# A decoder layer's router, tile by tile in place of pairs of tiles

## The reference, cut to what matters

```
x = layernorm(x + attn(x) @ Wo)                 # norm a
r = running sum over the batch of decay, ctx*ctx
x = layernorm(x + x * r)                        # norm b, written here in one product x * (r + 1)
h = rmsnorm(x) * norm_w
scores = softmax(h @ gate_w)                    # 32 experts
topk_w, topk_ids = top_k(scores, 4); topk_w /= sum(topk_w)
pos = rank of the token among those of the same expert, in token order
buf[expert, pos] = h, where pos < 256           # the rest is dropped
shared = silu(h @ shared_gate) * (h @ shared_up) @ shared_down
```

## Time and profile before

| | us |
|---|---|
| median of 3 runs | 1106.15 |
| lowest and highest | 1100.98, 1106.28 |
| the profiled execution | 1102.41 |
| its span | 1100.5 |

### The profile page before, as it was taken

The page is one execution under the profiler, slowest core; times in us unless marked ns, Lnnn a source line. Parts: engine busy times, 40 slices in busy tenths (PEclk is TensorE's granted clock), DMA queues, the critical chain, the costliest instruction groups (busy, mean ns, idle before and its releaser), DMA issues. The chain is left out here.

```text
span 1100.5 us, 18924 instructions
## 1 busy us (share of the span) xinstructions
PE 999.9 (91%) x6064; PEld 816.0 (74%) x6064; DVE 712.1 (65%) x2102; ACT 606.8 (55%) x1650; POOL 461.0 (42%) x473
## 2 busy tenths in 40 slices
PE   7999999998995699849899999988878889999996
PEld 5999899987883599727778888965444568877775
DVE  6666766672575366545655767645777557888886
ACT  3655566556222255436676776656775546555553
POOL 5777767861367444366211110210137214444321
PEclk9999999999997799969999999998988989999999
DMA  6731111000011599733401101001003011112101
GB/s 214 252 132 66 29 30 29 16 15 2 1 49 55 186 351 331 251 96 109 135 20 63 30 26 39 1 23 51 2 1 117 1 58 58 58 58 66 51 1 39
DMA packets 83784, 85.61 MB, mean 78 GB/s; under 512 B 8577, under 2 KB 75975, under 8 KB 83568
## 3 DMA queue, kind: packets, MB, share of 16 engines
q1 hardware_dynamic: 79776, 75.59, 21.1%
q0 software_dynamic: 3072, 7.34, 2.2%
q10 hardware_dynamic: 848, 1.57, 0.4%
HBM read 63.36 MB, written 22.02 MB: 78 GB/s over the span
## 5 line engine op out<-in xcount | busy, mean ns | idle before, releaser
L579 POOL TENSOR_TENSOR a_qk<-h,a_by_sin 128x512 f32<-128x512 f32 x64 | 81.9, 1279 | 5.0
L352 DVE CUSTOM_DVE_ANT_0 h<-a_score_ps,mask_bf 128x128 f32<-128x128 f32 (+1 forms) x128 | 40.8, 355 | 60.0 <-PE a_score_ps L345 60.0
L1296 POOL TENSOR_TENSOR a_w_l<-a_w,a_w_h 128x256 fp32r<-128x256 f32 x30 | 21.9, 729 | 111.2 <-ACT a_w_h L1489 111.0
L358 ACT ACTIVATE y_moe<-y_moe,a_nmax 128x128 f32<-128x128 f32 x64 | 25.6, 400 | 76.1 <-DVE a_nmax L352 76.1
L339 DVE COPY a_probsT<-a_turn_ps 128x384 f32<-128x384 f32 x64 | 34.9, 545 | 48.2 <-PE a_turn_ps L269 48.2
L1035 POOL TENSOR_TENSOR e_w_l<-e_w,e_w_h 128x512 fp32r<-128x512 f32 x32 | 40.8, 1275 | 52.7 <-ACT e_w_h L1103 52.7
L459 PEld LDWEIGHTS a_proj_ps<-a_w,xT 128*128 128x128 f32 x512 | 59.6, 192 | 1.3 <-issue 0.5
L80 PE MATMUL a_proj_ps<-a_x_l,a_w_h 128*128 128x512 f32 x128 | 56.9, 445 | 3.7 <-POOL a_w_l L584 3.6
L459 PE MATMUL a_proj_ps<-a_w,xT 128*128 128x128 f32 x512 | 59.8, 276 | 0.1
L759 PE MATMUL t_y_ps<-wo,attnT 128*128 128x256 f32 x256 | 57.6, 381 | 0.0
L2639 POOL TENSOR_TENSOR m_up_l<-m_up_w,m_up_h 128x1024 fp32r<-128x1024 f32 x8 | 19.5, 2438 | 89.3 <-ACT m_up_h L2611 89.3
(11 more groups left out here) (465 smaller groups left out, 3519.7 us busy)
## 6 DMA issues: line engine op xcount, KB each, us to landing
slots<-zeros SPq DMA_DIRECT2D x4, 2048.0 KB, 7.0
e_rows<-slots SPq DMA_DIRECT2D x32, 256.0 KB, 4.5
e_w<-in_L_ffn_w_dram SPq DMA_DIRECT2D x32, 256.0 KB, 4.7
out_slots<-e_out SPq DMA_DIRECT2D x32, 256.0 KB, 4.2
e_w<-in_L_ffn_w_dram SPq DMA_DIRECT2D x32, 128.0 KB, 4.1
a_w<-in_L_attn_w_q_dram SPq DMA_DIRECT2D x32, 128.0 KB, 2.2
m_up_w<-in_up_dram SPq DMA_DIRECT2D x8, 512.0 KB, 3.6
a_w<-in_L_attn_Wq_dram SPq DMA_DIRECT2D x16, 128.0 KB, 2.2
```

Of the source, the lines that this page charges most:

```text
L352: done = dve.tensor_tensor_reduce(self.probs[:, b, cells], self.score_ps[:, r, cells], self.k.mask_bf[:, cells], -1.0, 3e38, ALU.add, ALU. ...
L358: act.activation(self.probs[:, b, 0:P], self.probs[:, b, 0:P], ACT.Exp, bias=self.nmax[:, b, 0:1], scale=-1.0, accum_out=self.total[:, b, ...
L579: pool.tensor_tensor(qk[:, par, 0 if what == "q" else 1, half * HALF:(half + 1) * HALF], by_cos[:, r, :], by_sin[:, r2, :], ALU.add).then_ ...
```

## The change

The router's functions treat one tile each. `centre(t)` only finds the largest logit, and ScalarE's `exp` reads the logits in PSUM with it as bias, so that the subtraction (line 812) is gone. `place` makes its four products by one instruction over 128 elements. In VectorE's loop `choose(t - 2)` and `place(t - 2)` stand in every turn from t = 2, and `centre(t - 1)` from t = 1; all of `weigh` moves behind the loop. On TensorE `count(t - 3)` and `logits(t - 2)` stand in every turn. On GpSimd the scatters of tile t - 3 are issued in turn t from t = 3. Behind the loop the second shared product is cut into two halves, with the last count between them.

```diff
-                def logits(g):
-                    pe.wait_ge(k.hT_ready, 2 * g + 2)
-                    at_least(pe, centred, g)
-                    for t in (2 * g, 2 * g + 1):
+                def logits(t):
+                    pe.wait_ge(k.hT_ready, t + 1)
...
-                def shared_up(half):
-                    pe.wait_ge(k.hT_ready, 4 * half + 4)
+                def shared_up(half, j):
+                    if j == 0:
+                        pe.wait_ge(k.hT_ready, 4 * half + 4)
...
-                        if h == 11 and t >= 3 and t % 2:
-                            logits((t - 3) // 2)
-                        if h == 9 and t >= 4 and t % 2 == 0:
-                            count((t - 4) // 2)
+                        if h == 9 and t >= 3:
+                            count(t - 3)
+                        if h == 11 and t >= 2:
+                            logits(t - 2)
...
-                shared_up(0)
+                shared_up(0, 0)
+                shared_up(0, 1)
+                count(5)
                 turn_h(6)
-                count(2)
+                logits(6)
+                count(6)
                 turn_h(7)
-                logits(3)
-                shared_up(1)
-                count(3)
+                logits(7)
+                shared_up(1, 0)
+                count(7)
+                shared_up(1, 1)
...
-                def choose(g):
-                    ts = slice(2 * g, 2 * g + 2)
-                    dve.wait_ge(scored, g + 1)
-                    for t in (2 * g, 2 * g + 1):
-                        last = dve.max(top[:, t, :], score[:, t, :])
-                    chain(last)
-                    for t in (2 * g, 2 * g + 1):
-                        last = dve.max_index(top_at[:, t, :], top[:, t, :], score[:, t, :])
-                    chain(last)
+                def choose(t):
+                    dve.wait_ge(scored, t + 1)
+                    chain(dve.max(top[:, t, :], score[:, t, :]))
+                    chain(dve.max_index(top_at[:, t, :], top[:, t, :], score[:, t, :]))
...
                     residual(t)
-                    if t >= 3 and t % 2:
-                        choose((t - 3) // 2)
+                    if t >= 2:
+                        choose(t - 2)
                     if t >= 1:
                         rms(t - 1)
                     decay_gate(t)
-                    if t >= 3 and t % 2:
-                        place((t - 3) // 2)
+                    if t >= 2:
+                        place(t - 2)
+                    if t == NT - 1:
+                        centre(t - 1)
                     ln_b.gate(dve, t)
-                    if t >= 2 and t % 2 == 0:
-                        centre((t - 2) // 2)
+                    if 1 <= t < NT - 1:
+                        centre(t - 1)
                     ln_b.apply(dve, t)
-                    if t >= 4 and t % 2 == 0:
-                        weigh((t - 4) // 2)
+                choose(6)
                 rms(7)
-                centre(3)
-                choose(3)
-                place(3)
-                weigh(2)
-                weigh(3)
+                place(6)
+                for t in range(4):
+                    weigh(t)
+                centre(7)
+                choose(7)
+                weigh(4)
+                weigh(5)
+                place(7)
+                weigh(6)
+                weigh(7)
...
-                    if t == 4:
+                    if t == 3:
                         pool.wait_ge(k.zeroed, ZERO_DMAS * 16)
-                    if t >= 4:
-                        scatter(t - 4, (0, 1, 2))
+                    if t >= 3:
+                        scatter(t - 3, (0, 1, 2))
                     ln_b.power(pool, t)
-                    if t >= 4:
-                        scatter(t - 4, (3,))
+                    if t >= 3:
+                        scatter(t - 3, (3,))
                 rms_power(7)
-                for t in range(4, NT):
+                for t in range(5, NT):
                     scatter(t)
```

More of the change, by code:

```diff
@@ L731, in count @@
-                def count(g):
-                    pe.wait_ge(masked, g + 1)
-                    at_least(pe, slots_ready, g)
-                    for t in (2 * g, 2 * g + 1):
-                        for u in range(t + 1):
-                            last = pe.matmul(pos_ps[:, t * E0:(t + 1) * E0], (k.before_bf if u == t else k.ones_bf)[:, :],
-                                             mask[:, u, :], start=u == 0, stop=u == t)
-                    last.then_inc(counted, 1)
-                def shared_up(half):
-                    pe.wait_ge(k.hT_ready, 4 * half + 4)
[L742 to L748, removed]
+                def logits(t):
+                    pe.wait_ge(k.hT_ready, t + 1)
+                    for c in range(DC):
+                        last = pe.matmul(logit_ps[:, t * E0:(t + 1) * E0], k.hT[:, c, t * P:(t + 1) * P],
+                                         k.gate_w[:, c, :], start=c == 0, stop=c == DC - 1)
+                    last.then_inc(logits_done, 1)
@@ new lines, in count @@
+                def count(t):
+                    pe.wait_ge(masked, t + 1)
+                    for u in range(t + 1):
+                        last = pe.matmul(pos_ps[:, t * E0:(t + 1) * E0], (k.before_bf if u == t else k.ones_bf)[:, :],
+                                         mask[:, u, :], start=u == 0, stop=u == t)
+                    last.then_inc(counted, 1)
+                def shared_up(half, j):
+                    if j == 0:
+                        pe.wait_ge(k.hT_ready, 4 * half + 4)
+                        if half:
+                            pe.wait_ge(ln_a.summed, NT)
+                    for c in range(DC):
+                        last = pe.matmul(halves_ps[half][:, j, :], k.sh_up[:, c, j * I0:(j + 1) * I0],
+                                         k.hT[:, c, half * HALF:(half + 1) * HALF], start=c == 0, stop=c == DC - 1)
+                    if j:
+                        last.then_inc(up_done, 1)
@@ L828, in choose @@
                     with nc.allow_low_precision("0 and 1"):
-                        dve.tensor_reduce(mask[:, ts, :], chosen[:, ts, :, :].rearrange("p t k e -> p t e k"), AX,
+                        dve.tensor_reduce(mask[:, t, :], chosen[:, t, :, :].rearrange("p k e -> p e k"), AX,
                                           ALU.add).then_inc(masked, 1)
[L831 to L837, removed]
-                        last = dve.tensor_tensor(pos_of[:, :, j, :], chosen[:, ts, j, :], these, ALU.mult)
-                    chain(last)
-                    chain(dve.tensor_reduce(pos[:, ts, :], pos_of[:, :, :, :], AX, ALU.add))
-                    chain(dve.tensor_scalar(over[:, ts, :], pos[:, ts, :], float(CAP), 4.0 * SLOTS, ALU.is_ge, ALU.mult))
-                    chain(dve.tensor_tensor(to_f[:, ts, :], pos[:, ts, :], over[:, ts, :], ALU.add))
-                    dve.tensor_tensor(k.to_slot[:, ts, :], to_f[:, ts, :], base[:, ts, :], ALU.add
-                                      ).then_inc(slots_ready, 1)
@@ L846, in weigh @@
[L846 to L854 removed]
+                    chain(dve.tensor_scalar(base[:, t, :], expert[:, t, :], float(CAP), None, ALU.mult))
@@ L919, in _ @@
                 keep_hT(7)
[L920 removed]
+                exp(7)
                 act.wait_ge(projected, NT)
```

62 lines of the change are left out of this document (28 added, 34 removed).

## The result

Over seven runs each the changed kernel takes 1095.46 us in the median (1089.86 to 1097.36), the kernel before 1102.57 (1100.77 to 1106.28). The ratio is 0.9922, with a 95% interval of 0.9894 to 0.995. The change makes the kernel 0.8% faster, within the range stated and by nearly the amount forecast. In the profiled executions the span went from 1100.5 to 1094.5 us.

The account below looks back on a forecast made before the run. GpSimd was taken to bound the loop from turn 4 and the stage's end; 1.1 + 5.1 + 1.5 = 7.7 us, taken as 7.6, gave 1096.5 us between two baselines, with 1091 to 1103 for 8 in 10.

Parts of the forecast that it names:

- What sets the end: End of the expert stage: the first load of slots comes 2.92 us behind GpSimd's last scatter, VectorE finishing earlier.
- Four scatters, 5.1 us: GpSimd behind the loop: four scatters fewer at 1.27 us each, moved into turn 3's idle time, save 5.1 us.
- The loop, 1.1 us: Loop turns 4 to 7 fall to GpSimd's 8.1 us each, so the last `t_rvar` comes 1.1 us sooner.
- A single tile's price: VectorE in the loop: a 128-element instruction costs 0.29 us, one tile's choice 1.56 and its places 1.15.
- TensorE's round trip: In each loop turn `centre(t - 1)` waits for TensorE's logits, which are done 1.7 us before VectorE needs them.
- The rival of the lockstep: Loop turns 3 to 7: engines wait on each other, turns of 9.7 us or more make it slower; chance 0.08.
- The wait of 1.79 us: GpSimd behind the loop: slot numbers of tile 7 come 1.7 us before they are needed, saving 1.5 us.
- The shared expert: VectorE's tail behind the loop ends at 357.9 us, 1.5 us before the first load, and stays covered.
- a risk worth 1.4 us: At the stage's end, if the barrier needs all 2.92 us behind VectorE, 1.4 us of the gain are lost.
- Slow scatters beside VectorE: GpSimd's scatters slow to at most 1257 ns beside a busier VectorE, cutting the gain to 3 us; chance 0.10.
- The sum: Whole expert stage: loop, four scatters and removed wait give 7.7 us, taken as 7.6, with later work only shifted.
- two scales 3.7 us apart: Whole-kernel time: 1094.8 us from the profiled execution or 1098.5 from the runs' median; the middle, 1096.5, was taken.

Follow-up runs that it names:

- late_scatters: The changed kernel with GpSimd's scatters one tile later, none in turn 3 and sixteen behind the loop; 1101.58 us.
- fill_1: The changed kernel with one idle reduction over 256 elements behind `place` in each VectorE turn from 2 to 7; 1097.27 us.
- whole_product: The changed kernel with both halves of the second shared product ahead of the last counts; 1099.86 us.
- h_first: The changed kernel with h of the last tile computed ahead of the choice in VectorE's loop; 1099.65 us.
- fill_4: The changed kernel with four idle reductions behind `place` in each VectorE turn from 2 to 7; 1095.17 us.
- one_sooner: The changed kernel with each turn's single scatter taken from tile t - 2, from turn 2, eleven behind the loop; median 1092.01 us, ratio to before 0.9908.
- one_sooner_tail: As one_sooner, with the second shared product for tiles 4 to 6 before the last h and most weights among the last sums; median 1093.10 us, ratio 0.9912.

## Why the prediction was right, point by point

*What sets the end.* GpSimd's last scatter, by 2.92 us, before and after. Shown: late_scatters moves the load by the scatters' own time, fill_1 adds VectorE work for nothing. Of the fourteen profiles only whole_product has its load at another distance from the last scatter.

*Four scatters, 5.1 us.* Measured 5.1 in the trace; 4.92 by late_scatters, net of its turn 3.

*The loop, 1.1 us.* Measured 1.58, or 1.97 counted from each stage's start, and turns of 7.85 in place of my 8.1. The step that was mis-sized took 8.11 us as GpSimd's own work, as that turn had no wait. It held a loss that is no wait: 0.29 us in which line 137 ran beside VectorE's h. With the choice ahead of h in each turn the two no longer meet. h_first shows it. I also had turn 3 end 0.2 us later than before; it ended 0.8 later, of which 0.4 is a later start of the stage and 0.2 came from turn 2. The two misses have opposite signs.

*A single tile's price.* I took 0.29 us for 128 elements between 0.21 and 0.425; the record is 0.28 to 0.29 (lines 826 and 817). The choice took 1.53 us (331.35 to 332.88) against 1.56.

*TensorE's round trip.* No wait for logits or counts in the loop's turns. The rival of the lockstep is refuted: fill_4 puts 1.39 us more into each turn and costs 0.36.

*The wait of 1.79 us.* Tile 7's slot numbers came at 349.45, against 349.7 worked out, and their first scatter at 350.98, against 351.4. But the 1.53 us between aren't all margin. Where a scatter behind the loop had to wait, it started 0.79 to 0.80 us behind the write (before, whole_product, one_sooner and three more), so the margin was 0.73 us, not 1.7. The step held; one_sooner asks for the numbers 1.28 us sooner and runs out of the margin by 0.55, measured as a wait of 0.56.

*The shared expert.* VectorE's end at 356.13 against 357.9: the down product ran at a granted clock of 1.00, and I had taken the length from before, where it was 0.68. That is luck as far as the forecast goes. The shared expert stays cover, as forecast; in whole_product, with the product whole and the clock at 0.58, it is not. I had that only as a risk worth 1.4 us.

*Slow scatters beside VectorE.* None of the last twelve took over 1.06 us, so this rival is refuted for these scatters. The first scatter of the loop took 1.34 us, above the 1.26 that I had called the most. My price for the loop, 1.2 us for five turns of up to 0.6, doesn't follow from these figures, which give 3.0; nothing hung on it. The rule of the Trainium skill, page "SBUF — State Buffer", section "SBUF: two separate sides", also names a VectorE instruction with two inputs from SBUF against a GpSimd one that reads SBUF; the trace agrees with that half in h_first, 0.48 against 0.19 us, where line 137 ends 0.05 us behind h. I had weighed the rule for the wrong instruction.

*The sum.* 7.6 us forecast, 8.45 at the load, 8.84 as the stage's length. The medians differ by 7.1 us, the means of the seven runs by 8.8. I took 1096.5 us, the middle of two scales 3.7 us apart; 1095.46 came out. The seven runs before have a median of 1102.57, so the lower scale (1094.8) was the right one. That the middle of the two still came within 1.0 us is partly luck. In the profiled executions 2.4 us of the 8.45 don't arrive at the end; two profiles of the same kernel differ by 3.5 in that part. Is some of the gain given back behind the load all the same? Ten profiles with early loads have a rest of 728 to 739 us, 735.4 in the mean, four with late loads 729 to 734, 732.1 in the mean. The means of whole runs speak against it: they differ from before by 8.8 us (changed), 11.3 (one_sooner) and 10.2 (one_sooner_tail), where the stages differ by 8.8, 9.8 and 10.3. Why one execution has part of the attention at 1.2 GHz and another has not is open.

*Not tried alone.* The dropped subtraction (0.23 us for a pair) and the single product in `place` (0.3 us a tile by the prediction) were never taken back by themselves. With about 1.0 us of room in VectorE's turn they can hardly count in the loop; in the tail they belong to the 0.73 us of margin. That is argued, not shown.

## What to carry to other kernels

When an engine issues without a gap, count what it issues behind the last point where others still need it: moving an issue into a stretch where that engine is idle is worth nearly its whole pitch (4.92 of 5.1 us for four), as long as the data it needs are there when its place in the queue comes. Finer units on another engine are the price for that, and are free while that engine has room, which an idle filler measures in one run. A turn without a wait isn't yet an engine's least time; compare each record's duration with the shortest of its line.

## What the runs showed of the hardware

- GpSimd's one-column instruction at line 137 takes 0.19 us alone, and 0.26 or 0.48 beside some of VectorE's work. In the fourteen profiles it meets VectorE's h (two inputs from SBUF) 32 times: 29 times it took 0.48 to 0.49 us, once 0.30 and twice 0.19, and in these two h took 0.51 in place of 0.48.
- Indirect scatters of 128 rows behind the loop are issued every 1.27 to 1.28 us (0.97 and a gap of 0.30); single ones in the loop took up to 1.35. One that waited for its indices there starts 0.79 to 0.80 us behind their write. In thirteen of fourteen profiles 2.92 us lie between the last issue's end and the load that waits for it. In the fourteenth the load came 0.27 us behind VectorE's end.
- The same 16 records of the down product took 3.97, 5.41, 5.76 and 6.36 us in changed, before, one_sooner_tail and whole_product, at granted clocks of 1.00, 0.68, 0.66 and 0.58. TensorE had stood idle for 1.78, 3.70, 2.02 and 3.49 us just before, so the length of this last idle time doesn't put them in order.
